# Routing arithmetic of a gated cross-attention and expert layer in fewer VectorE instructions

## What is computed

```python
def xattn(features, masks, ctx, q_masks, Ws, W, w, b, Wcw, bcw, Wcb, bcb):
    h = tanh((ctx @ Ws)[:, None] + (features @ W)[:, :, None] + b)
    rho = einsum('bftd,d->bft', h, w[:, 0])
    rho = rho + (1.0 - q_masks)[:, None, :] * -1e30
    att = softmax(rho)
    txt_h = einsum('bft,btd->bfd', att, ctx)
    return tanh(txt_h @ Wcw.T + bcw) * features + tanh(txt_h @ Wcb.T + bcb)

def moe(x, router_w, w1, w2):
    probs = softmax(x @ router_w.T)
    vals, idx = top_k(probs, 2)
    for each expert e:
        weight = sum of vals where idx == e
        out += weight * (gelu(x @ w1[e].T) @ w2[e].T)

x = x + tanh(g_xattn) * xattn(layernorm(x), ...)
x = x + tanh(g_ffn) * moe(layernorm(x), ...)
```

## Time and profile before

| | us |
|---|---|
| median of 3 timed runs | 592.97 (592.93 to 594.25) |
| the profiled execution | 590.49 |
| its span, first to last instruction | 588.7 |
| PE busy | 523.3 (89%) |
| DVE busy | 359.1 (61%), 1190 instructions |
| ACT busy | 354.4 (60%) |
| POOL busy | 119.2 (20%) |
| mean granted TensorE clock | 0.944 |

### The profile page before, as it was taken

One profiled execution on the slowest core, in us unless ns is written; L12 is line 12 of the kernel. 1 busy time (PEld: TensorE's weight loads), 2 busy tenths in 40 slices (PEclk: granted clock), 3 DMA queues, 4 the chain that ended last, 5 costly groups with the idle time before them and its releaser, 6 DMA issues.

```text
span 588.7 us, 10199 instructions
## 1 busy us (share of the span) xinstructions
PE 523.3 (89%) x3432; PEld 338.6 (58%) x3433; DVE 359.1 (61%) x1190; ACT 354.4 (60%) x314; POOL 119.2 (20%) x96
## 2 busy tenths in 40 slices
PE   7887979665799898989899999999899999999994
PEld 5432323102255443545454555788799999999993
DVE  4889997898875799885799987376111111111110
ACT  1678999987998988999978999241011111111110
POOL 2000000050001253501243111136222222222222
PEclk9688989777899979999979999999999999999998
DMA  4101940055212026422128433349765555555541
GB/s 133 37 0 48 419 187 1 1 182 213 87 63 90 10 85 204 133 89 90 71 61 232 141 116 96 127 130 264 229 185 185 180 179 179 179 179 179 170 98 19
DMA packets 32937, 77.56 MB, mean 132 GB/s; under 512 B 4576, under 2 KB 25696, under 8 KB 26752
## 3 DMA queue, kind: packets, MB, share of 16 engines
q1 hardware_dynamic: 24848, 67.22, 33.1%
q0 software_dynamic: 7344, 9.72, 8.8%
q10 hardware_dynamic: 704, 0.09, 0.2%
HBM read 60.73 MB, written 16.29 MB: 131 GB/s over the span
## 4 chain that ended last, share of the span: by engine, by line
PE 60%; DVE 18%; ACT 10%; DMA 4%; issue 4%; SPq 3%; POOL 1%; POOLq 0%; DVEq 0%
PE h_ps L705 20%; PE y_bank L717 19%; PE rho L670 13%; DVE hbuf L872 8%; ACT hbuf L558 8%; PE misc L650 3%; DMA out<-x_res 2%; PE xsT_bank L659 2%; PE xsT_bank L693 1%; SPq L370 1%; SPq L371 1%; ACT hbuf L564 1%; PE h_ps L615 1%; DMA w_st<-in_w 1%; PE misc L641 1%
## 5 line engine op out<-in xcount | busy, mean ns | idle before, releaser
L558 ACT ACTIVATE hbuf<-hbuf 128x2048 f32<-128x2048 f32 (+2 forms) x160 | 247.3, 1594 | 38.8 <-DVE hbuf L872 38.4
L872 DVE TENSOR_SCALAR hbuf<-featT,txtb 128x512 f32<-128x512 f32 x525 | 216.2, 480 | 20.4 <-PE rho L670 19.2
L670 PE MATMUL rho<-hbuf,wpad 128*32 128x512 f32 x1232 | 175.0, 649 | 34.9 <-ACT hbuf L564 19.5
L705 PEld LDWEIGHTS h_ps<-xsT,w_st 128*128 128x128 f32 x1280 | 151.3, 194 | 28.3 <-issue 25.2
L705 PE MATMUL h_ps<-xsT,w_st 128*128 128x128 f32 x1280 | 157.4, 280 | 2.4 <-DMA w_st<-in_w 1.2
L717 PE MATMUL y_bank<-w_sb,hgT 128*128 x640 | 151.5, 387 | 2.3 <-DVE y_sb L1047 2.3
L717 PEld LDWEIGHTS y_bank<-w_sb,hgT 128*128 128x128 f32 x640 | 118.4, 192 | 38.3 <-issue 24.1
L587 ACT ACTIVATE hgT<-h_ps 128x1024 f32<-128x1024 f32 x40 | 40.8, 1019 | 165.5 <-PE h_ps L705 165.4
L511 POOL DMA_INDIRECT out<-y_sb,meta x40 | 69.0, 1726 | 300.4 <-DMA out<-y_sb,meta 126.9
L670 PEld LDWEIGHTS rho<-hbuf,wpad 128*32 128x32 f32 x1232 | 30.3, 113 | 121.2 <-ACT hbuf L564 46.2
L1033 DVE COPY xsT<-xsT_bank 128x256 f32<-128x256 f32 x40 | 16.9, 424 | 87.7 <-PE xsT_bank L693 87.7
(11 more groups left out here) (136 smaller groups left out, 189.7 us busy)
## 6 DMA issues: line engine op xcount, KB each, us to landing
w_st<-in_w SPq DMA_DIRECT2D x40, 1024.0 KB, 4.9
w_sb<-in_w SPq DMA_DIRECT2D x8, 1024.0 KB, 12.7
xs<-row_scratch SPq DMA_DIRECT2D x40, 132.5 KB, 4.5
row_scratch<-pad SPq DMA_DIRECT2D x33, 132.5 KB, 21.2
x_res<-in_x SPq DMA_DIRECT2D x4, 512.0 KB, 4.7
out<-x_res SPq DMA_DIRECT2D x4, 512.0 KB, 5.8
hgT<-in_x SPq DMA_DIRECT2D x3, 512.0 KB, 3.4
out<-y_sb,meta POOLq DMA_INDIRECT x40, 6.3
```

Of the source, the lines that this page charges most:

```text
L558: ins = s.activation(h, h, ACT.Tanh)
L670: ins = t.matmul(rho[q % 2][32 * j:32 * j + 32, :], wpad[:, c, 31 - r:63 - r], hbuf[:, k % HB, j, :], start=(k == 0), stop=(last and c == ...
L705: ins = t.matmul(h_ps[:, k * P:(k + 1) * P], w1_st[:, par, c, k * P:(k + 1) * P], xsT[:, c, :], start=(c == 0), stop=(c == DC - 1))
L872: ins = v.tensor_scalar(hbuf[:, k % HB, j:j + 1, :], featT[:, c, q:q + 1, :], txtb[:, c, bb, CG * r + j:CG * r + j + 1], None, ALU.add)
```

## The change

The steps keep their places; what they do is written with other instructions.
- The mask becomes a column: `mcol` has one value for each score row, and scores_out adds it in the copy out of PSUM. The step "mask" loses its addition; the maximum and the subtraction read PSUM. Four small loads, strided by single 4-byte elements, take the place of the replicated one, with a semaphore of their own (`mask_in`), behind the router's; `constants()` waits for them and makes `mcol` in four instructions.
- affine folds tanh(g) and the square into `scalar_tensor_tensor`: 7 instructions for 8, and `var2` is written by the fourth of them, not the last.
- `std` is multiplied into `lg_n` once, in "routed" of quarter 0, so `kappa` goes.
- `cum` and `worked` start at the regions' bases, so place and ranks add no `region`.

```diff
...
         cwb = sb("cwb", [P, B, 2, TP])
-        mneg = sb("mneg", [P, B, TP])
+        mask_i = sb("mask_i", [P, B], I32)
+        mcol = sb("mcol", [P, B])
         cols = sb("cols", [P, 4, DC])
...
         scale2 = sb("scale2", [P, TPQ])
-        kappa = sb("kappa", [P, TPQ])
         lg_n = sb("lg_n", [P, NTOK // P, E])
...
         slot = sb("slot", [P, 2, TPQ], I32)
-        region = sb("region", [P, E])
         tokid = sb("tokid", [P, NTOK // P], I32)
...
         wrep = x_res[:].rearrange("p t d -> p (t d)")[:, 0:2 * DC * P].rearrange("p (k c m) -> p k c m", k=2, c=DC)
-        mask_i = sc[:, 0:B, :].bitcast(I32)
         xn = rows[:, :, 0:D]
...
         text_in = sem("text_in")
+        mask_in = sem("mask_in")
         W_in = sem("W_in")
...
 
-        N_CONST = 4
+        N_CONST = 3
         POOL_CONSTS = 11
...
             act.dma_start(gs[:], scalars.partition_broadcast(P)).then_inc(consts_in, 16)
-            act.dma_start(mask_i[:, :, 0:T], mask.partition_broadcast(P)).then_inc(consts_in, 16)
             act.dma_start(rT[:], router).then_inc(consts_in, 16)
+            for j in range(CG):
+                act.dma_start(mask_i[32 * j:32 * j + len(range(j, T, CG)), :],
+                              mask[:, j:T:CG].rearrange("b r -> r b"), allow_slow_non_contiguous=True).then_inc(mask_in, 16)
             act.wait_ge(consts_in, 16 * N_CONST)
...
             v.memset(ctx4[:, :, T:TP], 0.0).then_inc(dve_const, 1)
-            v.memset(mneg[:, :, T:TP], FILL).then_inc(dve_const, 1)
+            v.memset(mcol[:], FILL).then_inc(dve_const, 1)
 
...
             def constants():
-                v.tensor_scalar(mneg[:, :, 0:T], mask_i[:, :, 0:T], 1.0, NEG, ALU.subtract,
-                                ALU.mult).then_inc(dve_const, 1)
+                dve.wait_ge(dve_const, 3)
+                dve.wait_ge(mask_in, 16 * CG)
+                for j in range(CG):
+                    at = slice(32 * j, 32 * j + len(range(j, T, CG)))
+                    ins = v.tensor_scalar(mcol[at, :], mask_i[at, :], 1.0, NEG, ALU.subtract, ALU.mult)
+                ins.then_inc(dve_const, 1)
                 dve.wait_ge(pool_const, POOL_CONSTS)
...
                 ins.then_inc(dve_const, 1)
-                v.tensor_scalar(region[:], iota8[:], float(CAP), None, ALU.mult)
-                v.memset(cum[:, 0, :], 0.0)
-                v.memset(worked[:], 0.0)
+                v.tensor_scalar(cum[:, 0, :], iota8[:], float(CAP), None, ALU.mult)
+                v.tensor_scalar(worked[:], iota8[:], float(CAP), None, ALU.mult)
                 v.memset(grain[:, 0:E], float(P))
...
                     dve.wait_ge(route_ps_ok, NQ)
-                    v.tensor_copy(lg_n[:].rearrange("p t e -> p (t e)"), xsT_bank[:, 0:NTOK // P * E]).then_inc(route_ok, 1)
+                    v.tensor_tensor(lg_n[:], xsT_bank[:, 0:NTOK // P * E].rearrange("p (t e) -> p t e", e=E),
+                                    std[:].unsqueeze(2).to_broadcast([P, NTOK // P, E]), ALU.mult).then_inc(route_ok, 1)
                     dve.wait_ge(route_ok, 1)
...
                     dve.wait_ge(h_used, NBLK * (q + 1))
-                    v.tensor_copy(rhoT, rho[q % 2][:]).then_inc(rhoT_ok, 1)
+                    v.tensor_scalar(rhoT, rho[q % 2][:], mcol[:, bb:bb + 1], None, ALU.add).then_inc(rhoT_ok, 1)
                 elif step == "mask":
...
                     scores = misc[0][:].rearrange("p (n j r) -> p n r j", n=TPQ, j=CG)[:, :, 0:RS, :]
-                    m = wide(mneg[:, bb if isinstance(bb, int) else bass.ds(bb, 1), :].rearrange(
-                        "p (r j) -> p r j" if isinstance(bb, int) else "p o (r j) -> p (o r) j", j=CG), TPQ, 1)
-                    link(v.tensor_tensor(sc[:].rearrange("p n (r j) -> p n r j", j=CG), scores, m, ALU.add))
-                    link(v.tensor_reduce(mx[:], sc[:], AX.X, ALU.max))
-                    v.tensor_tensor(sc[:], sc[:], wide(mx[:], TP), ALU.subtract).then_inc(shifted_ok, 1)
+                    link(v.tensor_reduce(mx[:], misc[0][:].rearrange("p (n j r) -> p n j r", n=TPQ, j=CG)[:, :, :, 0:RS],
+                                         AX.XY, ALU.max))
+                    top_score = mx[:].unsqueeze(2).unsqueeze(3).to_broadcast([P, TPQ, RS, CG])
+                    v.tensor_tensor(sc[:].rearrange("p n (r j) -> p n r j", j=CG), scores, top_score,
+                                    ALU.subtract).then_inc(shifted_ok, 1)
                 elif step == "gates":
...
                     dve.wait_ge(gate_t, 1)
-                    link(v.tensor_scalar(wt[:], wt[:], tg[:, 0:1], None, ALU.mult))
-                    link(v.tensor_tensor(ab[:, 0, :], wt[:, 0, :], rstd[:, at], ALU.mult))
-                    link(v.tensor_scalar(ab[:, 1, :], ab[:, 0, :], 1.0, None, ALU.add))
-                    v.tensor_tensor(ab[:, 2, :], ab[:, 0, :], mv[:, at, 0], ALU.mult)
-                    link(v.tensor_tensor(square[:], ab[:, 1, :], ab[:, 1, :], ALU.mult))
-                    v.tensor_tensor(ab[:, 2, :], wt[:, 1, :], ab[:, 2, :], ALU.subtract)
-                    link(v.tensor_tensor(square[:], square[:], mv[:, at, 1], ALU.mult))
+                    link(v.scalar_tensor_tensor(ab[:, 0, :], wt[:, 0, :], tg[:, 0:1], rstd[:, at], ALU.mult, ALU.mult))
+                    link(v.scalar_tensor_tensor(square[:], ab[:, 0, :], 1.0, mv[:, at, 1], ALU.add, ALU.mult))
+                    link(v.scalar_tensor_tensor(square[:], ab[:, 0, :], 1.0, square[:], ALU.add, ALU.mult))
                     v.tensor_scalar(var2[:], square[:], EPS, None, ALU.add).then_inc(var2_ok, 1)
+                    v.tensor_scalar(ab[:, 1, :], ab[:, 0, :], 1.0, None, ALU.add)
+                    link(v.tensor_tensor(ab[:, 2, :], ab[:, 0, :], mv[:, at, 0], ALU.mult))
+                    link(v.scalar_tensor_tensor(ab[:, 2, :], wt[:, 1, :], tg[:, 0:1], ab[:, 2, :], ALU.mult, ALU.subtract))
                 elif step == "scale":
...
                     link(v.tensor_tensor(scale2[:], ab[:, 1, :], rstd2[:], ALU.mult))
-                    link(v.tensor_tensor(kappa[:], scale2[:], std[:, TPQ * q:TPQ * (q + 1)], ALU.mult))
-                    link(v.tensor_tensor(lg[:], lg_n[:, TPQ * q:TPQ * (q + 1), :], wide(kappa[:], E), ALU.mult))
+                    link(v.tensor_tensor(lg[:], lg_n[:, TPQ * q:TPQ * (q + 1), :], wide(scale2[:], E), ALU.mult))
                 elif step == "x2":
...
                                          .rearrange("p (t e) -> p t e", e=E), ALU.add))
-                    link(v.tensor_tensor(pos[:], pos[:], wide(region[:], TPQ, 1), ALU.add))
                     v.tensor_copy(cum[:, 0, :], cum[:, TPQ, :])
...
                     dve.wait_ge(rows_ok, q + 1)
-                    v.tensor_tensor(pad_r[:], region[:], cum[:, 0, :], ALU.add).then_inc(padrow_ok, 1)
+                    v.tensor_copy(pad_r[:], cum[:, 0, :]).then_inc(padrow_ok, 1)
                 elif step == "ranks":
...
                                       key[:].unsqueeze(2).to_broadcast([P, E, E]), ALU.is_gt))
-                v.scalar_tensor_tensor(start[:], worked[:], -float(PADROW), region[:], ALU.add, ALU.add)
+                v.tensor_scalar(start[:], worked[:], -float(PADROW), None, ALU.add)
                 tlink(v.tensor_reduce(first[:, E:2 * E], beats[:], AX.X, ALU.add))
...
```

## The result

| | before | after |
|---|---|---|
| median, us (8 runs each, side by side) | 593.26 (591.53 to 594.92) | **587.16** (585.99 to 590.52) |
| ratio after to before | | 0.9901 [0.988, 0.9922] |
| the profiled execution, us | 590.49 | 587.28 |
| its span | 588.7 | 584.9 |
| mean granted clock | 0.944 | 0.949 |

The change gains 6.1 us of medians.

A forecast was written before the change was run, and what follows sets the result against it. PE holds 60% of the chain; DVE settlings, ACT and PE stretches follow one another, so DVE's time counts in settlings. Gains 0.98, 0.79, 0.59 and 0.22 make 2.58: 590.49 becomes 587.91, plus 2.48 gives 590.4 us; range 589.0 to 592.6.

The forecast's parts named there:

- From the profiled execution to the median: Last step of the forecast: the median lies 2.48 us above the profiled execution, carried over to give 590.4.
- the sum: Gains of quarters 1 to 3 and the last settling, together 2.58 us, taking the profiled execution from 590.49 to 587.91.
- The loads of the mask: Start of the span: four small strided loads for the replicated 77 KB one, priced 0, at most 0.64 us gained.
- The mask: Step "mask" in DVE's settlings, ahead of ACT's exponential: 0.45, 0.26 and 0.39 us gained in quarters 1 to 3.
- The maximum at twice its time: Rival in step "mask": the maximum over PSUM with gaps takes 0.49 us more, giving 591.5; chance 0.08.
- affine, scale, place: DVE's settlings: affine 0.11 us (quarters 1, 2), scale 0.20 (quarters 1 to 3), place 0.22 (quarters 1, 2, last settling).
- Quarter 3: Third quarter's settling: 0.59 us gained, 0.39 from the mask and 0.20 from scale; affine and place 0.
- Last settling: Final stretch that DVE nearly fills: 0.22 us gained from place; mask, affine and scale 0, covered by waits.
- Quarter 0: Column and count starts cost about 0.4 us more, covered by 1.1 us before PE's turn: price 0.
- The late mask: Rival at the start: DVE waits at 20.2 us for four loads landing in turn, 2.7 us lost, 593.1; chance 0.05.
- The clock falls: Rival in full PE stretches: pieces at 1.2 GHz; one fall 593.9, chance 0.10; two falls 597.4, chance 0.07.
- two feared stretches: PE's full stretches from 256.7 and 321.9 us, where falls of the clock in both would lose 7.0 us.

The follow-up runs named there:

- e1: The kernel before, run once more unchanged, for the span and clock of every run: 592.84 us, ratio 0.9988.
- e5: The kernel before with the new mask alone (small loads, column, copy, maximum), arithmetic as before: 589.9 us, ratio 0.992.
- e7: The kernel before with 20 instead of 12 warm-up matmuls, loads as before: 591.35 us, ratio 0.995.
- e14: The changed kernel with filler matmuls in PE's wait for the picks, ahead of the counts of quarters 2 and 3: 586.25 us, ratio 0.9912.
- e15: The changed kernel with 16 warm-up matmuls and filler matmuls in PE's wait for the picks: 586.83 us, ratio 0.9914.
- e2: The changed kernel with the replicated mask load put back ahead of the router's, its data unused: 587.2 us, ratio 0.9916.
- e4: The kernel before with the new arithmetic alone (affine, scale, starts of the counts, routed), mask as before: 590.13 us, ratio 0.9963.
- e9: The changed kernel with the replicated mask load put back in its old place, measured a second time: 590.35 us, ratio 0.9948.
- e11: The kernel before with the new arithmetic alone, mask as before, measured a second time: 589.5 us, ratio 0.9935.
- e6: The changed kernel with 4 instead of 12 warm-up matmuls at the start: 591.19 us, ratio 0.9935.

## Why the prediction fell short, by its steps

**From the profiled execution to the median.** This is the step that failed, together with the next, and the two are in the main one shortfall seen from two sides, not to be added. For the profiled execution the sum gave 587.91, and the profile of after measured 587.28. But the prediction then carried the 2.48 us between the profile and the median of before over as a constant, and that was none: behind the change the median lies 0.12 under the profile. The spans of e1 have a median 2.2 us above the profiled 588.7, and of the seven profiles with the replicated load in front five have the clock fall in PE's wait, which that one had not. The change takes the long wait away, so most of the 2.48 goes with it. That the sum came so near for the profiled pair is in part luck: the start gave more than forecast, and the middle of quarter 1 took 0.61 back.

**The loads of the mask.** Priced at 0, with 0.64 as an end that took the load's bytes as its share of the traffic. In one pair of profiles the start gained 1.03, over thirteen profiles 3.3. Two things were missed. The replicated load held the context up by more than its bytes (its 77 KB in front, the context 1.8 us later); whether its small pieces are the reason was not tried. And PE's wait for the context is a place where the execution can go either way: where the clock has risen within the warm-up, the long wait lets it fall again ahead of the products. The profile of before is one of the two in seven where the clock rose late and held. That one profile could not show the split, but the wait of 2.30, with a warm-up in front of it that is there for the clock, stood in it and was the place to ask.

**The mask.** Right: 0.45, 0.26 and 0.39 were forecast up to the exponential, and it comes 0.47, 0.25 and 0.39 earlier behind the copy of rho. The maximum at twice its time did not happen (492 ns). The Trainium skill, "VectorE: DVE Perf Modes", section on the TRN2 errata, would by the estimate that the prediction took from it have put some 0.065 us more on each of the two that now read PSUM; L896 with 492 against 486 and L899 with 491 against 492 do not show it.

**affine, scale, place.** Right in kind: the sums end the wait and not POOL, and the steps of kappa and region are gone from the chain. Quarter 1 was given as 0.98 and quarter 2 as 0.79, they measured 1.02 and 0.93; the excess of quarter 2 lies between the tanh of the gates and top2, 3.08 us for 3.55 before, 0.47 where 0.31 was given. Quarter 3: 0.59 given, 0.5 where PE's up half ends last, 1.04 where it does not; the prediction let x_out wait for PE there, but in the profile of before it starts at 301.74 with no wait in front, as DVE's own sums and PE's turn end together; which of the two comes last is not fixed. Last settling: 0.22 given, 0.30 measured. Together 2.58 forecast, 2.8 to 3.3 measured.

**Quarter 0.** The column's four instructions at 19 us, behind the block's sum and with no wait for the mask:

```profile
18.77 0.48 DVE L877 TENSOR_SCALAR hbuf<-featT,txtb 128x512 f32<-128x512 f32 x1
19.17 0.68 DVE L820 TENSOR_SCALAR mcol<-mask_i 20x2 f32<-20x2 int32 x4
```

The late mask did not come, and they cost nothing that can be seen.

**The clock falls.** Neither of the two feared stretches shows a fall (1.00 from 254 to 280 and from 318 to 375 us above). One short fall came elsewhere, in the tail. What the rival had right is that falls of the clock move this kernel by microseconds; it looked for them in other places and as a loss, and the largest one here, at the start, is a fall that the change takes away.

The sum by what was measured: start some 3 (2.6 to 3.6), settling 2.8 to 3.3, the middle of quarter 1 between a small loss and 1.4, less up to 2 in the tail; the medians say 6.1 (5.8 to 6.6 in the sets that have after).

## What to carry to other kernels

Look at a wait of TensorE at the start in more than one execution: here its length varied by over a microsecond from run to run, and what runs behind it took 2.47 us for 1.32. A small load that is replicated over all partitions is worth trying behind the loads on which the first work waits; here moving it alone gave 2.6 us. When a change is worth 1%, compare the spans of many executions with the one that was profiled before its offset is taken as a constant, and read a stretch in the profiles of all variants: those that do not vary carry the argument.

## What the runs showed of the hardware

- The same 12 warm-up matmuls take 4.31 to 5.49 us in different executions, for the clock rises at 4.1 us in one and not before 7.4 in another; the end of the warm-up, not only the landing of the context, sets the length of the wait behind it.
- Where the clock had risen within the warm-up, TensorE did the eight products in 1.32 us behind waits of 0.60 to 1.43 (after, e5, e7, e14, e15), and in 2.47 behind waits of 2.79 to 3.48 (e1, e2, e4, e9, e11), in which the clock fell. The Trainium skill, "TensorE: Matmul & The Clock Gate", Part 1, says that the number of slow matmuls at a kernel's start changes from run to run, and that this is under 1% of a typical span. The runs agree with both, 3.3 of 590 us; here it was half of the gain.
- In e6 the granted clock from 6 to 20 us is given as 1.00, although the products took 2.47. Its trace has no record of the clock before 16.3 us, and the column counts what has no record as full. So the durations, and not that column alone, have to be read at the start.
- Four DVE instructions on 20 or 19 partitions that start at partitions 0, 32, 64 and 96 take 0.68 us, 0.17 each, without overlap, where independent ones on all partitions start 0.07 to 0.08 apart. The Trainium skill, "VectorE: DVE Perf Modes", section "Two Vector instructions with no wait between them", says that an instruction whose input starts in another group of 32 partitions than the last one's is held until that has finished; the trace agrees.
